# Linear attention and a LoRA mixture-of-experts FFN on one core: stage-1 products split 384 + 280, denominators and spreading on strips of the array, DVE order of a tile rewritten

## The chip, the core and the metric

The kernel runs on one core of a Trainium2 chip. TensorE (PE) multiplies, VectorE (DVE), ScalarE (ACT) and GpSimd (POOL) work beside it, SyncE (SP) issues nearly all DMAs. The metric is the device time of the whole program in microseconds (us); less is better.

## What is computed

`x` is 2 batches of 1024 tokens of 512 numbers, all float32. The reference, cut to what matters:

```python
xn = layernorm(x)
Q, K, V = heads(xn @ wq.T + bq), heads(xn @ wk.T + bk), heads(xn @ wv.T + bv)   # 16 heads of 32
Q, K = elu(Q) + 1.0, elu(K) + 1.0
KV = einsum('bhsd,bhse->bhde', K, V)
QKV = einsum('bhsd,bhde->bhse', Q, KV)
QK_sum = einsum('bhsd,bhd->bhs', Q, K.sum(axis=-2))
attn = (QKV / (QK_sum[..., None] + 1e-8)) @ wo.T + bo

scores = sigmoid(xn @ W_router)                      # 8 experts, two best of scores + bias
w = one_hot(topk_idx) * topk_scores / topk_scores.sum()
gate = xn @ W_gate + shared_lora(xn) + expert_lora(xn, w)
up   = xn @ W_up   + shared_lora(xn) + expert_lora(xn, w)
hidden = silu(gate) * up                             # 1376 wide
out = x + attn + hidden @ W_down + shared_lora(hidden) + expert_lora(hidden, w)
```

## The kernel before, in words

Every float32 operand of a large product is split into a rounded part (`_h`, type fp32r, written by ACT) and a remainder (`_l`, written by DVE as a subtraction). A product is then three matmuls, h times h, h times l, l times h (`product`), 512 columns wide as a rule.

**Stage 1** goes over 16 tiles of 128 tokens. For a tile `t`, PE computes the keys K (12 matmuls of 512 columns), transposes the next tile's normalised tokens (`transpose_tokens(t + 1)`), transposes the LoRA inputs of tile `t - 2` (`lora_transposed`), computes the values V (12 x 512) and the LoRA and router columns A (12 x 152), and multiplies keys by values of tile `t - 1` (`keys_by_values`: 16 small float32 matmuls of 33 columns, written to four strips of 32 partitions in turn). PE starts a tile's K only when DVE has written that tile's `xt_l` (`tokens_lo`, semaphore `xtl_done`).

Each engine has its queue in the order in which the code is written, and an instruction that waits holds all behind it. The parts that matter here:

- DVE in a tile `t`: `compare(t - 1)` (four small operations on the router scores), `select(t - 1)` (waits for POOL's rank), `kb` (keys plus bias, out of PSUM), the statistics of tile `t + 2`, `kf` (waits for ACT's exponential), `tokens_lo(t + 1)`, `lora_weighted(t - 1)` (`zs`, `zf`; waits for POOL's `wtok`), `normalise(t + 2)` (`xn`; waits for POOL's `rstd`), `lora_lo(t - 1)` (`zst`), the copy `zraw` of the A product, and in every second tile the sum `kvacc`.
- POOL in a tile: `rstd` of tile `t + 2`, then `route(t)`: `rden`, the rank (`eq`, `gt`, `rank`), after `select` seven more dependent operations (`ssum` to `wtok`). So `rstd` of tile `t + 2` stands behind the whole of `route(t - 1)`.
- ACT: `krelu`, `kexp`, `xt_h` of the next tile, `zt` (`lora_out`), `vf` (values), `zst` (`lora_hi`), `rexp`.

**Stage 2** goes over 4 groups of 512 tokens. In a group `g`, PE does `queries(g)` (12 matmuls for each of 4 chunks; the first chunk ahead, at the end of group `g - 1`), `attention(g - 1)` in two halves of 24 matmuls, and between the halves `denominators(g)`: four float32 matmuls that accumulate Q times the key sums of 16 heads in 16 partitions of bank 2. DVE then adds the epsilon and takes the reciprocal, ACT rounds it, DVE writes the remainder (`rr`), and PE spreads 16 rows to 4 x 128 (`expand`: one matmul a chunk, chunks 0 and 1, then `queries(g + 1, (0,))`, then chunks 2 and 3, since only two banks are there). DVE multiplies (`scaled`), ACT rounds, POOL takes the remainder (`qn_l`), and attention follows in the next group. In group 0, 20 matmuls that do nothing (`keep_busy`) run while DVE takes the reciprocal. In the last group, DVE also splits the first weights of stage 3 (`split_up(0, 0, 1)`), after `attention(g - 1, (0, 1))` and before the reciprocal.

**Stage 3** is the FFN, 4 groups of 11 chunks: gate and up products, silu, down products. The change leaves it as it is but for its first chunk.

## Time and profile before

| | us |
|---|---|
| median of 3 runs | 721.21 |
| lowest and highest | 720.41 and 721.88 |
| the profiled execution, its own time | 720.7 |
| its span, first to last instruction | 718.9 |

The profile is of one execution. It gives the busy time of each engine, the waits of each engine with what ended them, the chain of work that ended last, and each instruction with its start and duration. Matmuls overlap, so what a matmul costs on PE is read from the chain, where each piece has the time that it adds, and not from its own duration. "issue" is time in which an engine waited for nothing that the profile shows. The granted clock of TensorE is the full one in all 40 slices.

### The profile page before, as it was taken

The numbers are of one execution on the slowest core, as the hardware profiler recorded it, in microseconds if no ns is written. First come the engines' busy times: TensorE is split into PE (matmuls) and PEld (weight loads), VectorE is DVE, ScalarE is ACT, GpSimd is POOL, SyncE is SP. The second block draws the span as 40 slices with busy tenths as digits, with TensorE's granted clock in tenths as the row PEclk, the third lists the DMA queues.
The fourth block names the chain that finished last, engine by engine and source line by source line (L and its number), as shares of the span: only waits on it lengthen the run. The fifth ranks groups of instructions, "written<-read, shape, count | busy, mean of one in ns | idle before, by whom it ended". The sixth has DMA issues, their size and how long they took to land.

```text
span 718.9 us, 10792 instructions
## 1 busy us (share of the span) xinstructions
PE 701.2 (98%) x3690; PEld 563.2 (78%) x3690; DVE 376.2 (52%) x715; ACT 260.7 (36%) x402; POOL 122.3 (17%) x293
## 2 busy tenths in 40 slices
PE   7999999989999999999999999999999999999997
PEld 5788888876776677888888888888888888888886
DVE  5666556677575675444427444336534435544434
ACT  4344334564331432333333333324333224323322
POOL 3554555420642651000000000000000000000000
PEclk9999999999999999999999999999999999999999
DMA  7756656326746635000010500001600001300001
GB/s 241 270 194 195 202 192 210 125 111 251 274 142 236 221 131 217 18 0 0 0 49 37 208 0 0 0 4 54 233 0 0 0 0 58 117 0 0 0 0 60
DMA packets 22755, 72.79 MB, mean 101 GB/s; under 512 B 2688, under 2 KB 2944, under 8 KB 20688
## 3 DMA queue, kind: packets, MB, share of 16 engines
q1 hardware_dynamic: 22560, 72.24, 28.4%
q0 software_dynamic: 176, 0.30, 0.2%
q8 instruction: 11, 0.18, 0.1%
q14 instruction: 8, 0.07, 0.0%
HBM read 51.56 MB, written 20.97 MB: 101 GB/s over the span
## 4 chain that ended last, share of the span: by engine, by line
PE 90%; DVE 4%; issue 2%; POOL 2%; ACT 1%; DMA 1%; SPq 0%; DVEq 0%; POOLq 0%; ACTq 0%
PE bank L1115 19%; PE bank L1116 19%; PE bank L1117 19%; PE bank L1328 17%; PE bank L1303 6%; PE bank L1315 4%; PE bank L1228 2%; DMA w_raw<-in_wkT 1%; PE bank L1180 1%; PE bank L1132 1%; PE bank L1152 1%; PE bank L1144 1%; PE bank L1236 1%; PE bank L1344 0%; PE bank L1346 0%
## 5 line engine op out<-in xcount | busy, mean ns | idle before, releaser
L1115 PE MATMUL bank<-x,up_h 128*128 (+1 forms) x352 | 137.5, 391 | 2.1 <-DVE qf L980 1.2
L1116 PE MATMUL bank<-x,up_h 128*128 (+1 forms) x352 | 137.3, 390 | 0.0
L1117 PE MATMUL bank<-x,up_l 128*128 (+1 forms) x352 | 137.0, 389 | 0.0
L1048 DVE TENSOR_TENSOR hf<-bank,silu 128x512 f32<-128x512 f32 x44 | 30.4, 692 | 162.3 <-issue 142.6
L1115 PEld LDWEIGHTS bank<-x,up_h 128*128 128x128 f32 x352 | 66.1, 188 | 18.8 <-issue 2.1
L597 ACT ACTIVATE hid_h<-hf 128x512 fp32r<-128x512 f32 x44 | 27.8, 632 | 142.9 <-DVE hf L1048 142.9
L1117 PEld LDWEIGHTS bank<-x,up_l 128*128 128x128 f32 x352 | 66.1, 188 | 14.1
L1116 PEld LDWEIGHTS bank<-x,up_h 128*128 128x128 f32 x352 | 66.1, 188 | 13.8
L793 DVE TENSOR_TENSOR up_l<-up_raw,up_h 128x1024 fp32r<-128x1024 f32 x45 | 55.6, 1235 | 31.4 <-ACT up_h L597 31.4
L1328 PE MATMUL bank<-dn_h,hid_h 128*128 128x512 f32 x176 | 69.5, 395 | 0.0
L1328 PE MATMUL bank<-dn_l,hid_h 128*128 128x512 f32 x176 | 69.1, 392 | 0.0
L1328 PE MATMUL bank<-dn_h,hid_l 128*128 128x512 f32 x176 | 68.9, 392 | 0.0
L597 ACT ACTIVATE up_h<-up_raw 128x1536 fp32r (+1 forms) x45 | 66.0, 1474 | 1.5 <-DVE qf L949 1.5
L750 ACT ACTIVATE silu<-bank 128x512 f32<-128x512 f32 x44 | 26.3, 597 | 101.6 <-PE bank L1303 101.5
L1303 PE MATMUL bank<-z,up_h 128*128 128x512 f32 x176 | 54.2, 389 | 0.0
L793 DVE TENSOR_TENSOR hid_l<-hf,hid_h 128x512 fp32r<-128x512 f32 x44 | 30.5, 692 | 33.8 <-ACT hid_h L597 33.8
L597 ACT ACTIVATE dn_h<-dn_raw 128x592 fp32r (+1 forms) x44 | 30.8, 699 | 43.0 <-PE bank L1315 31.4
L793 DVE TENSOR_TENSOR up_h<-up_raw,up_h 64x256 fp32r<-64x256 f32 x90 | 39.5, 439 | 0.6
L793 DVE TENSOR_TENSOR dn_l<-dn_raw,dn_h 128x592 fp32r<-128x592 f32 x44 | 34.1, 775 | 10.4 <-ACT dn_h L597 9.3
L1328 PEld LDWEIGHTS bank<-dn_h,hid_l 128*128 128x128 f32 x176 | 33.0, 188 | 7.6
L1328 PEld LDWEIGHTS bank<-dn_h,hid_h 128*128 128x128 f32 x176 | 33.0, 187 | 7.4
L1328 PEld LDWEIGHTS bank<-dn_l,hid_h 128*128 128x128 f32 x176 | 33.1, 188 | 7.1
(167 smaller groups left out, 1228.3 us busy)
## 6 DMA issues: line engine op xcount, KB each, us to landing
x<-scr_x SPq DMA_DIRECT2D x8, 2048.0 KB, 7.5
up_raw<-in_ffn_up SPq DMA_DIRECT2D x11, 768.0 KB, 5.5
scr_x<-xt SPq DMA_DIRECT2D x16, 512.0 KB, 4.4
xin<-in_x SPq DMA_DIRECT2D x16, 256.0 KB, 5.8
scr_z<-zt SPq DMA_DIRECT2D x16, 256.0 KB, 2.2
x3r<-in_x SPq DMA_DIRECT2D x16, 256.0 KB, 3.5
scr_att<-x3r SPq DMA_DIRECT2D x16, 256.0 KB, 2.1
z<-scr_z SPq DMA_DIRECT2D x4, 1024.0 KB, 5.0
```

What stands on the lines that cost most here:

```text
L597: return nc.scalar.activation(dst, src, ACT.Copy)
L750: nc.scalar.activation(silu[:], ps_g[:], ACT.Silu).then_inc(silu_done, 1)
L793: return nc.vector.tensor_tensor(dst, a, b.bitcast(F32), ALU.subtract)
L1048: nc.vector.tensor_tensor(hf[:], ps_u[:], silu[:], ALU.mult).then_inc(h_done, 1)
L1115: nc.tensor.matmul(dst, lh, rh, start=start, stop=False, **kw)
L1116: nc.tensor.matmul(dst, lh, rl, start=False, stop=False, **kw)
L1117: return nc.tensor.matmul(dst, ll, rh, start=False, stop=stop, **kw)
L1132: last = nc.tensor.transpose(ps_xt[:, k * P:(k + 1) * P], xn[:, k * P:(k + 1) * P], ident[:])
L1228: last = nc.tensor.matmul(ps_den[0:HEADS, :], kcur[:, c, :], qf[:, c, :], start=(c == 0), stop=(c == KD - 1))
L1303: last = nc.tensor.matmul(dst[:], up_h[:, s, col:col + P], z4[:, :, a * 2 + b, :], start=False, stop=(b == 1))
L1315: d = nc.tensor.matmul(ps_zd[0:DNR, :], w[:, s, D:], h[:, s, :], start=(first and i == 0), stop=(last and i == 2), skip_group_check=True)
L1328: d = nc.tensor.matmul(ps_out[j][:], h[:, s, cols], w[:, s, 0:D], start=(first and i == 0), stop=False, skip_group_check=True)
```

## The change

Stage 1: V and A now stand in one set of 664 columns, and are computed as 384 columns (`va`, three quarters of V) and 280 columns (`vz`, the last quarter of V and A) in two banks; `lora_transposed(t - 2)` stands between them, no longer ahead of V. ACT reads the values in two pieces, the second after DVE's `zraw`. `zraw` has two buffers. DVE's order of a tile is another one: `kb` ahead of `compare` and `select`, and `lora_weighted` and `lora_lo` at the end of the tile, behind `normalise` and `zraw`. The split of `wo` is one quarter in each of the last four tiles in place of two in each of the last two. The loop over tile pairs is one turn shorter, with two more tiles written out.

Stage 2: the denominators of chunk `c` go to partitions 32c to 32c + 31 (heads in rows 0 to 15 and again in 16 to 31), with four separate matmuls of 32 columns of weights; the key sums `kcur` are made once a batch on POOL straight from `kvacc`. The reciprocal and the rest work on 128 partitions, the remainder is made with a mask column `lomask` (one more small load), and `expand` takes 32 partitions a chunk as its contraction, into four banks, all four at once. PE's groups 1 and 2 are written out. In the last group the large part of `split_up` stands between the two halves of `attention(g - 1, (0, 1))` on DVE and the small part behind `attention(g - 1, (2, 3))`, with a semaphore `upb_done` of its own.

```diff
-            for dst, name in ((hmask, "headmask"), (hcol, "headcol"), (hrow_raw, "headrow"), (bdn_raw, "b_dn")):
+            for dst, name in ((hmask, "headmask"), (hcol, "headcol"), (hrow_raw, "headrow"), (lomask, "lomask"), (bdn_raw, "b_dn")):
...
+            def key_sums(b):
+
+                pool.wait_ge(kvacc_done, (b + 1) * TB // 2 + 1)
+                tt(kcur[:, b], hcol[:], kvacc[:, b, :, DK:AUG].to_broadcast([P, KD, DK]), ALU.mult).then_inc(kcur_done, 1)
...
 # ACT, stage 1
+                act.wait_ge(va_ready, t + 1)
+                round_to(vf[:, s, 0:KD - 1, :, 0:DK], ps_va.rearrange("p (k h n) -> p k h n", h=HC, n=DK)).then_inc(va_done, 1)
                 if behind(t, 2):
                     lora_out(t - 2)
-
-                act.wait_ge(v_ready, t + 1)
-                round_to(vf[:, s, :, :, 0:DK], ps_v[:].rearrange("p (k h n) -> p k h n", k=KD, h=HC)).then_inc(vf_done, 1)
+                act.wait_ge(zraw_done, t + 1)
+                round_to(vf[:, s, KD - 1, :, 0:DK], ps_vz[:, 0:P].rearrange("p (h n) -> p h n", n=DK)).then_inc(vf_done, 1)
+                nc.scalar.activation(rexp[:], zraw[:, s, NZ - E:], ACT.Exp, scale=-1.0).then_inc(rexp_done, 1)
                 if behind(t, 1):
                     lora_hi(t - 1)
-
-                act.wait_ge(zraw_done, t + 1)
-                nc.scalar.activation(rexp[:], zraw[:, NZ - E:], ACT.Exp, scale=-1.0).then_inc(rexp_done, 1)
...
 # DVE, stage 1
+                dve.wait_ge(k_ready, t + 1)
+                wait(dve, kf_done, t)
+                nc.vector.tensor_tensor(kb[:], ps_k[:], bk_b[:], ALU.add).then_inc(kb_done, 1)
                 if not first:
                     compare(t - 1)
-                    select(t - 1)
-
-                dve.wait_ge(k_ready, t + 1)
-                nc.vector.tensor_tensor(kb[:], ps_k[:], bk_b[:], ALU.add).then_inc(kb_done, 1)
                 if first:
                     tokens_lo(1, 1)
                 if ahead(t, 2):
                     stats_of(t + 2, s, half + 1)
...
+                if not first:
+                    select(t - 1)
 
                 dve.wait_ge(kexp_done, t + 1)
...
-                if not first:
-                    lora_weighted(t - 1)
                 if ahead(t, 2):
                     normalise(t + 2, s)
+                dve.wait_ge(vz_ready, t + 1)
+                nc.vector.tensor_copy(zraw[:, s], ps_z).then_inc(zraw_done, 1)
                 if not first:
+                    lora_weighted(t - 1, 1 - s)
                     lora_lo(t - 1)
-                dve.wait_ge(z_ready, t + 1)
-                nc.vector.tensor_copy(zraw[:], ps_z[:, 0:NZ]).then_inc(zraw_done, 1)
                 if s == 0 and not first:
                     key_values(t - 1, half - 1)
...
 # DVE, stage 2
-                    attention(g - 1, (0, 1))
-                if then is not None:
-                    then()
+                    attention(g - 1, (0,))
+                    if last:
+                        split_up_w(0, 0, 1).then_inc(upl_done, 1)
+                    attention(g - 1, (1,))
...
-                nc.vector.reciprocal(den[0:HEADS, :], den[0:HEADS, :]).then_inc(rden_done, 1)
+                nc.vector.reciprocal(den, den).then_inc(rden_done, 1)
...
-                sub(rr[DK:DK + HEADS, :], den[0:HEADS, :], rr[0:HEADS, :]).then_inc(rr_done, 1)
+                nc.vector.scalar_tensor_tensor(rr[:], rr[:].bitcast(F32), lomask[:], den, ALU.mult, ALU.add
+                                               ).then_inc(rr_done, 1)
...
+                if last:
+                    split_up_b(0, 0).then_inc(upb_done, 1)
...
 # PE, stage 1
+                wait(pe, va_done, t)
+                tile_of(ps_va, s, va_h[:, :, 0:VA], va_l[:, :, 0:VA], split_before=KD if first else None
+                        ).then_inc(va_ready, 1)
                 if behind(t, 2):
                     lora_transposed(t - 2)
-                wait(pe, vf_done, t)
-                tile_of(ps_v[:], s, wv_h, wv_l, split_before=KD if first else None).then_inc(v_ready, 1)
...
-                tile_of(ps_z[:, 0:NZ], s, a_h, a_l).then_inc(z_ready, 1)
+                tile_of(ps_vz, s, va_h[:, :, VA:], va_l[:, :, VA:]).then_inc(vz_ready, 1)
...
 # PE, stage 2
-                    last = nc.tensor.matmul(ps_den[0:HEADS, :], kcur[:, c, :], qf[:, c, :], start=(c == 0), stop=(c == KD - 1))
+                    last = nc.tensor.matmul(ps_den[c * DK:(c + 1) * DK, :], kcur[:, g // GB, c, :], qf[:, c, :], start=True, stop=True)
...
-                for c in cs:
-                    wait(pe, qn_done, g * KD + c - 1)
-                    nc.tensor.matmul(ps_exp[c % 2][:], hrow[:, c, :], rr[:], start=True, stop=True).then_inc(exp_ready, 1)
+                wait(pe, qn_done, g * KD)
+                for c in range(KD):
+                    strip = slice(c * DK, (c + 1) * DK)
+                    nc.tensor.matmul(ps_exp[c][:], hrow[strip, :], rr[strip, :], start=True, stop=True).then_inc(exp_ready, 1)
...
                     gate_or_up(g, n, 0, 1, first=True)
-                    expand(GROUPS - 1, (2, 3))
                     gate_or_up(g, n, 0, 0)
```

Three places of the instruction streams. The first is DVE in a tile of stage 1. In a row stand the line, the operation, what is written and what is read, and what it waits for; `eq` and `gt` are left out, `zf`, `zs` and `zst` are the LoRA inputs. Before:

```order
L829 RECIPROCAL score<-rden_106 128x8 [waits rden1_done]
...
L841 SCALAR_TENSOR_TENSOR sel<-rank,score 128x8 [waits rank_done]
...
L868 TENSOR_TENSOR kb<-bank,bk_b 128x512 [waits k_ready]
...
L880 SCALAR_TENSOR_TENSOR kf<-kb,kexp 128x512 [waits kexp_done]
L793 TENSOR_TENSOR xt<-bank,xt 128x512 [waits xth_done]
L847 TENSOR_SCALAR zs<-zraw 128x16 [waits route_done]
...
L851 TENSOR_TENSOR zf<-zraw,wtok 128x64 x2
L806 TENSOR_SCALAR xn<-xin,mv,rstd 128x512 [waits xt_ready,ln_rstd]
L793 TENSOR_TENSOR zst<-zf,zst 128x2x64 [waits zhi_done,zf_done]
L793 TENSOR_TENSOR zst<-zs,zst 128x2x8
L892 COPY zraw<-bank 128x152 [waits z_ready]
```

The same place on DVE in the changed kernel:

```order
L869 TENSOR_TENSOR kb<-bank,bk_b 128x512 [waits kf_done]
L833 RECIPROCAL score<-rden_103 128x8 [waits rden1_done]
...
L845 SCALAR_TENSOR_TENSOR sel<-rank,score 128x8 [waits rank_done]
L884 SCALAR_TENSOR_TENSOR kf<-kb,kexp 128x512 [waits kexp_done]
L797 TENSOR_TENSOR xt<-bank,xt 128x512 [waits xth_done]
L810 TENSOR_SCALAR xn<-xin,mv,rstd 128x512 [waits xt_ready,ln_rstd]
L892 COPY zraw<-bank 128x152 [waits vz_ready]
L851 TENSOR_SCALAR zs<-zraw 128x16 [waits route_done]
...
L855 TENSOR_TENSOR zf<-zraw,wtok 128x64 x2
L797 TENSOR_TENSOR zst<-zf,zst 128x2x64 [waits zhi_done,zf_done]
L797 TENSOR_TENSOR zst<-zs,zst 128x2x8
```

`kb` has moved ahead of the comparison, `select` stands right before `kf`, and `zs`, `zf` and `zst` have moved behind `xn` and `zraw`.

The second place is PE in group 0 of stage 2, from the denominators (`kcur`) through the filler (`ident_sb`) and the spreading (`hrow`) to the first query products of group 1 (`wq_h`). Before:

```order
L1228 MATMUL bank<-qf,kcur 16x512 x3
...
L1180 MATMUL bank<-ident_sb 128x128 x20
L1236 MATMUL bank<-rr,hrow 128x512 [waits rr_done,hrow_done]
L1236 MATMUL bank<-rr,hrow 128x512
L1115 MATMUL bank<-x_52,wq_h 128x512 [waits qmax_done,x3_in]
...
L1236 MATMUL bank<-rr,hrow 128x512 [waits qn_done,rr_done]
L1236 MATMUL bank<-rr,hrow 128x512 [waits qn_done]
```

PE at the same place in the changed kernel:

```order
L1242 MATMUL bank<-qf,kcur 32x512 x3
...
L1193 MATMUL bank<-ident_sb 128x128 x20
L1251 MATMUL bank<-rr,hrow 128x512 [waits rr_done,hrow_done]
L1251 MATMUL bank<-rr,hrow 128x512 x3
L1127 MATMUL bank<-x_52,wq_h 128x512 [waits qmax_done,x3_in]
```

The spreading is now in one place, ahead of the query products.

The third place is DVE in the last group of stage 2, with the sums of the attention (`x3r`), the split of stage 3's first weights (`up_l`, `up_h`), the reciprocal and the scaling (`qf<-qf,bank`). Before:

```order
L956 TENSOR_TENSOR x3r<-x3r,bank 128x512 [waits xbo_done,att_ready] x2
L793 TENSOR_TENSOR up_l<-up_raw,up_h 128x1024 [waits uph_done]
L793 TENSOR_TENSOR up_h<-up_raw,up_h 64x2x128
L793 TENSOR_TENSOR up_h<-up_raw,up_h 32x2x128
L967 TENSOR_SCALAR qexp<-bank 16x512 [waits den_ready]
L969 RECIPROCAL qexp<-qexp 16x512 [waits dene_done]
L793 TENSOR_TENSOR rr<-qexp,rr 16x512 [waits rrh_done,rden_done]
L956 TENSOR_TENSOR x3r<-x3r,bank 128x512 [waits xbo_done,att_ready] x2
L980 TENSOR_TENSOR qf<-qf,bank 128x512 [waits exp_ready] x4
```

The same place on DVE in the changed kernel:

```order
L959 TENSOR_TENSOR x3r<-x3r,bank 128x512 [waits xbo_done,att_ready]
L797 TENSOR_TENSOR up_l<-up_raw,up_h 128x1024 [waits uph_done]
L959 TENSOR_TENSOR x3r<-x3r,bank 128x512 [waits xbo_done,att_ready]
L991 TENSOR_SCALAR qexp<-bank 128x512 [waits den_ready]
L993 RECIPROCAL qexp<-qexp 128x512 [waits dene_done]
L996 SCALAR_TENSOR_TENSOR rr<-rr,lomask_sb,qexp 128x512 [waits rrh_done,rden_done]
L959 TENSOR_TENSOR x3r<-x3r,bank 128x512 [waits xbo_done,att_ready] x2
L797 TENSOR_TENSOR up_h<-up_raw,up_h 64x2x128
L797 TENSOR_TENSOR up_h<-up_raw,up_h 32x2x128
L1007 TENSOR_TENSOR qf<-qf,bank 128x512 [waits exp_ready] x4
```

The large piece of the split now stands between two attention sums, the two small pieces right before the scaling.

## Rows read from the trace of the kernel before

**Rows 1.** The page, part 1: busy time, share of the span, instructions.

```profile
PE 701.2 (98%) x3690; PEld 563.2 (78%) x3690; DVE 376.2 (52%) x715; ACT 260.7 (36%) x402; POOL 122.3 (17%) x293
```

**Rows 2.** Waits of PE: line, releaser, us in total, times, longest.

```profile
PE bank L1115 <- DVE xt L793: 2.4, 2, 1.5
...
PE bank L1115 <- DVE qf L980: 1.2, 1, 1.2
```

**Rows 3.** Chain that ended last, stage 1: start us, us added, what.

```profile
34.25 0.23 PE bank L1116
...
35.90 0.11 PE bank L1117
36.01 0.39 PE bank L1144 x32
...
44.72 0.24 issue
...
149.21 0.47 PE bank L1115
```

**Rows 4.** Timeline of DVE, tiles 1 to 3: start, us, line, out<-in, [idle <-releaser].

```profile
24.52 0.68 DVE L868 TENSOR_TENSOR kb<-bank,bk_b 128x512 f32<-128x512 f32 x1
...
30.03 0.20 DVE L829 RECIPROCAL score<-rden 128x8 f32<-128x8 f32 x1 [0.56 <-POOL rden L531]
...
32.56 0.17 DVE L841 SCALAR_TENSOR_TENSOR sel<-rank,score 128x8 f32<-128x8 f32 x1 [1.73 <-POOL rank L538]
32.66 0.69 DVE L868 TENSOR_TENSOR kb<-bank,bk_b 128x512 f32<-128x512 f32 x1
...
34.80 0.69 DVE L880 SCALAR_TENSOR_TENSOR kf<-kb,kexp 128x512 f32<-128x512 f32 x1 [0.51 <-ACT kexp L632]
...
36.01 0.17 DVE L847 TENSOR_SCALAR zs<-zraw 128x16 f32<-128x16 f32 x1
...
36.37 0.55 DVE L806 TENSOR_SCALAR xn<-xin,mv,rstd 128x512 f32<-128x512 f32 x1
37.11 0.29 DVE L793 TENSOR_TENSOR zst<-zf,zst 128x128 fp32r<-128x128 f32 x1 [0.20 <-ACT zst L597]
...
37.41 0.31 DVE L892 COPY zraw<-bank 128x152 f32<-128x152 f32 x1
37.63 0.28 DVE L818 TENSOR_TENSOR kvacc<-kvacc,bank 128x132 f32 x1
38.34 0.20 DVE L829 RECIPROCAL score<-rden 128x8 f32<-128x8 f32 x1 [0.43 <-POOL rden L531]
```

**Rows 5.** Timeline of ACT in tile 2.

```profile
36.47 0.42 ACT L597 ACTIVATE zst<-zf 128x256 fp32r<-128x256 f32 x1 [0.24 <-DVE zf L851]
```

**Rows 6.** Timeline of POOL in tile 2.

```profile
30.91 0.32 POOL L534 TENSOR_TENSOR eq<-eq,earlier_sb 128x64 f32<-128x64 f32 x1 [0.91 <-DVE eq L836]
...
32.33 0.20 POOL L538 TENSOR_TENSOR rank<-gt 128x8 f32<-128x8 f32 x1
32.81 0.20 POOL L541 TENSOR_TENSOR ssum<-sel 128x4 f32<-128x4 f32 x1 [0.28 <-DVE sel L841]
...
34.90 0.66 POOL L547 TENSOR_TENSOR wtok<-sel,ssum 128x8 f32 x1 [0.18 <-POOL ssum L546]
```

**Rows 7.** Timeline of PE in tile 1, right behind K.

```profile
21.40 0.60 PE L1132 MATMUL bank<-ident_sb,xn 128*128 128x128 f32 x4
```

**Rows 8.** Chain that ended last, stage 2: start us, us added, what.

```profile
194.53 3.54 PE bank L1228 x8
...
207.22 0.45 PE bank L1236 x2
...
266.50 0.23 PE bank L1115
```

**Rows 9.** Timeline of DVE, stage 2, last group.

```profile
251.56 0.68 DVE L967 TENSOR_SCALAR qexp<-bank 16x512 f32<-16x512 f32 x1 [0.95 <-PE bank L1228]
```

**Rows 10.** Timeline of POOL, stage 2, last group.

```profile
259.78 2.53 POOL L582 TENSOR_TENSOR qn_l<-qf,qn_h 128x512 fp32r<-128x512 f32 x2 [14.26 <-ACT qn_h L597]
```

More of the change, by code:

```diff
@@ L52 @@
 RSCALE = 1.0 / R
-STAGE2_LOADS = 8
-WO_HALF = {TILES - 2: (0, 1), TILES - 1: (2, 3)}
+STAGE2_LOADS = 9
+WO_PART = {TILES - KD + k: k for k in range(KD)}
 ROUTE_STEPS = 10
@@ L343, in tiles @@
             body(1, 0, 1)
[L344 removed]
+            with eng.Fori(0, TILES // 2 - 3) as p:
                 body(2 * p + 2, p + 1, 0)
                 body(2 * p + 3, p + 1, 1)
[L347 removed]
+            for t in range(TILES - 4, TILES):
                 body(t, t // 2, t % 2)
@@ L983, in group @@
                         m_lo(1, (2, 3))
-                    if c == 3 and then is None:
+                    if c == 3 and not last:
                         queries(g + 1, (0,))
@@ L1093, in late_group @@
                 chunk(n + FC - 1, FC - 1, 0, last=True)
-            group(GROUPS - 1, then=lambda: split_up(0, 0, 1))
+            group(GROUPS - 1, last=True)
             split_up(1, 1, 2)
@@ L1276, in group3 @@
                 attention(g - 1, (2, 3))
-                expand(g, (0, 1))
+                expand(g)
                 if more:
                     queries(g + 1, (0,))
-                    expand(g, (2, 3))
-            with pe.Fori(1, GROUPS - 1) as g:
+            for g in range(1, GROUPS - 1):
                 group3(g)
```

143 lines of the change are left out of this document (73 added, 70 removed).

## The prediction

> **What bounds the kernel now.** I read the busy table first, then the waits of PE, then the chain of work that ended last, and last the instructions of single tiles. PE is busy for 701.2 of 718.9 us, 98% [rows 1], so the plain reading is that whatever shortens PE's work shortens the kernel. Its waits are few: the two for `xt` make 2.4 us, the one for the scaled queries (`qf`, line 980) 1.2 [rows 2]. But this says only that the other engines are in time for PE as it is now, not by how much. That must be read from a tile of stage 1. On DVE one tile's first comparison starts at 30.03 and the next one's at 38.34, 8.31 later [rows 4], and on PE the keys by values end at 36.40 and again at 44.72, 8.32 later, with 0.24 of issue at every second tile [rows 3]: 8.44 a tile. In this tile the copy `zraw` starts right behind `zst` and not when its product is there, and `xn` right behind POOL's `rstd`. So a circle through DVE, POOL and ACT turns nearly as slowly as PE: PE is the bound with a tenth or two of a microsecond to spare. Whether the change shortens that circle decides stage 1.
>
> **Stage 1, PE's work.** In the chain a 512-column matmul adds 0.23 us and a 152-column one 0.11 [rows 3], that is 0.45 and 0.74 ns a column: narrow ones pay more. The 12 pairs cost 12 x 0.344 = 4.13 us a tile. 384 + 280 columns are not in the trace. At 0.45 ns a column the pair costs 0.30; at the other end the 280 could cost 0.74 ns a column, 0.21, and the 384 as much as a 512, and nothing would be gained. I take 0.31, nearer to the wide row, since both widths are over half of 512: 0.4 us a tile, 6 us in all, if nothing else binds.
>
> **Stage 1, the circle.** With `kb` at 0, in the changed order:
> - `kb` 0.68, the next starts 0.09 before its end, as `kvacc` does behind `zraw` [rows 4]: 0.60. Comparison to POOL's `eq`: 30.03 to 30.91 = 0.88; `eq` to the end of `rank`: 30.91 to 32.53 = 1.62 [rows 4, 6]; `select` 0.03 later. Sum 3.13.
> - `select` to `xn` is 32.56 to 36.37 = 3.81 [rows 4]. In it POOL does `ssum` to `wtok`, then `rstd` of tile `t + 2`. `wtok` took 0.66 and ended at 35.56, just behind the end of `kf` at 35.49, against 0.20 for other small POOL operations: it was held while `kf` ran [rows 4, 6]. Now `kf` follows `select` at once and holds the first `ssum` instead (+0.40) and frees `wtok` (-0.46). I keep 3.75.
> - `xn` to `zraw` 0.46 (0.55 less 0.09), `zraw` to `zs` 0.22, `zs` to ACT's `zst` 0.46 (36.01 to 36.47), ACT's to DVE's `zst` 0.64, and 0.30 to the next instruction [rows 4, 5]. Sum 2.08.
> Together 8.96 us; in every second tile `kvacc` and the wait for its end add 0.31. Mean 9.12 a tile against 8.4.
>
> What makes it longer is the order. Before, `kb`, the statistics and `kf` ran in the shade of POOL's routing, and the LoRA steps ahead of `xn` in the same shade. Now `kb` stands ahead of the comparison (+0.60), and `zs` to `zst` stand behind `xn`, which itself waits for POOL to finish the whole route. The second `zraw` buffer takes `rexp` and `rden` out of the circle (0.93 from `zraw` to the next comparison, 37.41 to 38.34), but that is less. PE waits for `xt` once a tile, some 1.2 us: the shortened products and the later LoRA transposes win nothing, and the wait is the price of the order. ACT's second half of `vf` comes 0.35 behind `zraw` and doesn't bind.
>
> Sum: tile 1's `kb` stood at 24.52 behind `select`, though K had ended at 21.40 [rows 4, 7]. It moves to about 21.3, since the first tile's products are a little shorter. Then 7 x 8.96 + 6 x 9.27 = 118.3 to `kb` of tile 14; 0.3 each for the quarters of `wo_l` in tiles 12 and 13, which hold POOL's rank; 0.2 at each of 5 loop ends, as on PE (0.24 of "issue") [rows 3]. That is 141.2. Tile 14 has no `xn`, but `zs` waits for `wtok`: 3.44 to `select`, 2.94 to `wtok`, 0.6 more since `kvm` runs beside POOL, 1.4 to the end of `zst`, 0.3 for `kvacc`: 8.7. In tile 15 `wtok` ends at 6.4, ACT's `zst` starts at 6.9, behind it ACT rounds the transposed heads (to 7.9), DVE takes the remainder (to 8.65), PE starts: 8.9. So the first product of stage 2 starts at 158.8 in place of 149.21 [rows 3]: **+9.6 us**. An error of 0.15 in the circle is 2 us here.
>
> **Stage 2, denominators.** 4 matmuls, 8 pieces, add 3.54 us [rows 8], 0.885 each, on the path in each of 4 groups. On four strips they can run side by side. Bounds: 0.885 (all at once) and 3.54 (in turn). The nearest row are the keys by values, 32 pieces of 33 columns to four strips in 0.39 [rows 3]. At the denominators' 0.86 ns a column they would take 0.91 in turn, so strips do overlap, 2.3 times, and by that the denominators would be 1.5. But those pieces are so short (12 ns each) that issue may set them. I take 1.05, near the lower bound: -2.5 us a group. DVE works on 128 partitions in place of 16, which costs nothing by the rows (0.68 for 16 x 512, 0.69 for 128 x 512 [rows 4, 9]). Its chain from the denominators to `rr` is as long as before and lies beside the same work, attention's second half or the filler, so all of the gain reaches the end: **-10.0**. The Trainium skill (TensorE: Matmul & The Clock Gate, "Part 3: Packing small matmuls") gives three column strips of N = 512 a measured 2.38 times and four row strips 3.07 times; by the latter, an estimate, the denominators would be 1.15 and the sum 0.4 us worse.
>
> **Stage 2, spreading.** Two matmuls add 0.45 in the stream [rows 8], so four 0.90. In strips, with 32 partitions each, between 0.23 and 0.90, and no row shows strips of the contraction. I take 0.35: -0.55 in groups 0 to 2, **-1.65**. `key_sums` on POOL is free: between two routes for batch 0, and behind the last route for batch 1, whose user is group 2. The added small load goes to SP long before its use.
>
> **Last group.** From DVE's first step on the denominators at 251.56 to the first attention product behind the gate at 266.50 are 14.94 us [rows 8, 9], the 1.2 of wait in it. Afterwards, counted from that step: the scaling, which stood at about 6.75, starts 0.85 later, behind the two small splits of 256 columns (some 0.42 each, estimated from 0.68 for 512), at 7.6. POOL's first `qn_l` starts 1.48 behind it (scaling and rounding), at 9.1, and the four take 1.27 each (2.53 for two [rows 10]), to 14.2: attention starts at 14.3, **-0.6**. The wait for the queries goes, and POOL's is late next. The split's large piece would have delayed the reciprocal, now that the denominators are short, by up to 1.1; its move avoids that.
>
> **Sum.** +9.6 - 10.0 - 1.65 - 0.6 = -2.65. The profiled execution's own time is 720.7, so 718.05; the median of the runs is 0.5 above it, so **718.6** as a median.
>
> **Rivals.**
> - *Stage 1 is held by PE after all* (my circle is too long, say because POOL isn't held by `kf`, or `xn` waits less). At the old 8.4 a tile stage 1 costs nothing and the time is 709; with the full 0.4 a tile and K of tile 2 starting 2 us earlier it is 701. For it: 98% busy. Against it: `xn` right behind `rstd` in rows of before. 14%.
> - *The circle is still longer.* The Trainium skill (SBUF — State Buffer, "SBUF: two separate sides") says that DVE and GpSimd share a port pair that the first comer locks for its whole instruction; the trace agrees for `wtok` behind `kf` [rows 4, 6]. If more of POOL's operations are held than I count (the rank by the statistics, the last ones by `xt_l`), 0.3 a tile adds 4: 722.5, on the other side. It decides from 0.2 a tile. 13%.
> - *Strips don't overlap*: the four denominators keep 3.54 and the spreading 0.9. Then stage 2 gains 0.6 only and stage 1's loss stands: 730. Against it the keys by values. Half an overlap: 723. 9%.
> The forecast's own case has 64%, 714.5 to 722.
>
> **How the numbers follow.** A run of this kernel can tell 0.2%, 1.4 us, from no change. Faster (below 719.8): 0.52 of the 0.64 and all of the first rival, 0.66. Same: 0.10 and a part of the others, 0.16. Slower: 0.18. The range leaves out the lower half of the first rival and the upper half of the third: 709 to 724.
>
> **What would show it.** Right: PE in stage 1 waits for `xt` once a tile, together 12 to 18 us; comparison to comparison on DVE about 9.1; the product after the last tile at 159; `kcur` pieces about 1.05 a group in the chain, and a group of stage 2 some 3 us shorter. Wrong: tiles of 8.0 to 8.4 without waits (first rival), or `kcur` pieces over 2 us (third).

## Result: 0.45% slower, and the profile after

The changed kernel takes **725.84 us** as a median of 7 runs (724.54 to 726.18); the kernel before takes 721.92 in 7 runs beside them (720.41 to 723.62). The ratio, of the two means, is 1.0045, with a 95% interval of 1.0029 to 1.0061. Forecast were 718.6, 0.4% faster than the median of 721.21 that was known then, and it became 0.45% slower. The profiled execution spans 723.8 us, before 718.9; this difference, 4.9, is larger than that of the medians, 3.9. One reason is under "The clock" below: the profiled execution of before is one of its quick ones.

Waits of PE in the changed kernel (engine, line waited for: us in total, times, longest); before, `xt` made 2.4 us in two waits [rows 2]; "..." stands for lines left out, here and in all that follows:

```profile
PE bank L1127 <- DVE xt L797: 18.6, 15, 1.8
...
PE bank L1164 <- DVE zst L797: 2.5, 1, 2.5
PE bank L1127 <- POOL qn_l L591: 1.5, 1, 1.5
...
PE bank L1127 <- DMA x<-scr_x: 0.7, 1, 0.7
PE bank L1127 <- DVE qf L1007: 0.4, 1, 0.4
```

So PE waits for `xt` in 15 of the 16 tiles, as forecast. What PE does in between is shorter, also as forecast. Timeline of PE in tile 2: the second and the eleventh product of 384 columns, and the same of 280:

```profile
30.93 0.34 PE L1128 MATMUL bank<-va_l,xt 128*128 128x384 f32 x1
...
32.51 0.34 PE L1128 MATMUL bank<-va_l,xt 128*128 128x384 f32 x1
...
33.43 0.29 PE L1128 MATMUL bank<-va_l,xt 128*128 128x280 f32 x1
...
34.59 0.29 PE L1128 MATMUL bank<-va_l,xt 128*128 128x280 f32 x1
```

Nine steps take 1.58 and 1.16 us: 0.176 and 0.129 a product, a pair 0.304 (estimate 0.31, before 0.344 [rows 3]).

The circle of the same tile. First DVE, then POOL (start, duration; in brackets the idle time ahead and what ended it); compare [rows 4 to 6]:

```profile
31.79 0.69 DVE L869 TENSOR_TENSOR kb<-bank,bk_b 128x512 f32<-128x512 f32 x1
...
34.93 0.17 DVE L845 SCALAR_TENSOR_TENSOR sel<-rank,score 128x8 f32<-128x8 f32 x1 [0.80 <-POOL rank L546]
35.02 0.68 DVE L884 SCALAR_TENSOR_TENSOR kf<-kb,kexp 128x512 f32<-128x512 f32 x1
...
38.84 0.55 DVE L810 TENSOR_SCALAR xn<-xin,mv,rstd 128x512 f32<-128x512 f32 x1 [2.54 <-POOL rstd L520]
...
39.53 0.16 DVE L851 TENSOR_SCALAR zs<-zraw 128x16 f32<-128x16 f32 x1
...
40.63 0.29 DVE L797 TENSOR_TENSOR zst<-zf,zst 128x128 fp32r<-128x128 f32 x1 [0.67 <-ACT zst L603]
...
41.24 0.69 DVE L869 TENSOR_TENSOR kb<-bank,bk_b 128x512 f32<-128x512 f32 x1
```

```profile
35.18 0.58 POOL L549 TENSOR_TENSOR ssum<-sel 128x4 f32<-128x4 f32 x1 [0.28 <-DVE sel L845]
...
37.66 0.21 POOL L555 TENSOR_TENSOR wtok<-sel,ssum 128x8 f32 x1 [0.18 <-POOL ssum L554]
37.99 0.19 POOL L518 TENSOR_TENSOR vare<-mv,epsln 128x1 f32<-128x1 f32 x1
38.26 0.55 POOL L520 TENSOR_TENSOR rstd<-vare,mhalf 128x1 f32<-128x1 f32 x1
```

`kb` to `kb` is 9.45 us in this even tile, 9.22 in tile 1 (22.57 to 31.79); the mean of tiles 1 to 13 is 9.46, and the kernel before needed 8.32 there. DVE stands idle 2.54 us ahead of `xn`, because POOL computes `rstd` only behind the route, and the LoRA steps (`zs` to `zst`, with 0.67 of idle for ACT) stand behind that wait.

Stage 2. PE's four denominators, DVE's reader of them, and the spreading, in group 2; compare [rows 8, 9]:

```profile
231.23 1.07 PE L1242 MATMUL bank<-qf,kcur 128*32 128x512 f32 x8
232.23 0.50 PE L1127 MATMUL bank<-m_h,qn_h 128*128 128x512 f32 x1
```

```profile
232.37 0.69 DVE L991 TENSOR_SCALAR qexp<-bank 128x512 f32<-128x512 f32 x1 [0.34 <-PE bank L1242]
```

```profile
238.01 0.51 PE L1251 MATMUL bank<-rr,hrow 32*128 32x512 f32 x4
238.45 0.50 PE L1127 MATMUL bank<-x,wq_h 128*128 128x512 f32 x1
```

The denominators take 1.00 of PE's stream (3.54 before), the spreading 0.44 (0.90). A group takes 23.80 us from spreading to spreading (214.21 to 238.01), before 26.74.

Where the 4.9 us come from, by marks in the two profiled executions:

| stretch | before | after | difference | forecast |
|---|---|---|---|---|
| start to `kb` of tile 1 | 24.52 | 22.57 | -1.95 | -3.2 |
| to the first product of stage 2 | 124.69 | 140.18 | +15.49 | +12.8 |
| to the first denominators | 18.41 | 19.59 | +1.18 | 0 |
| to the first spreading | 9.41 | 7.28 | -2.13 | -2.5 |
| to the second denominators | 17.43 | 17.81 | +0.38 | -0.55 |
| to the fourth denominators | 53.46 | 47.63 | -5.83 | -6.1 |
| to DVE's last addition to `x3r` | 29.50 | 27.57 | -1.93 | -3.1 |
| to the end | 441.48 | 441.17 | -0.31 | 0 |
| sum | 718.9 | 723.8 | +4.9 | -2.65 |

Two groups of errors are to be explained: stage 1 (the first two stretches) is 3.9 us worse than forecast, stage 2 is 3.6 worse.

### The profile page after: what moved, and what is told of

It is laid out like the page before. It is cut to its first block, busy times and chain, and to the rows that moved or that the text cites. A ratio compares the mean times of both kernels' runs of the same rounds, so it can differ in the third digit from the quotient of the medians.

```text
span 723.8 us, 10757 instructions
## 1 busy us (share of the span) xinstructions
PE 688.7 (95%) x3690; PEld 559.9 (77%) x3690; DVE 375.7 (52%) x712; ACT 260.9 (36%) x418; POOL 121.3 (17%) x291
## 4 chain that ended last, share of the span: by engine, by line
PE 63%; issue 15%; POOL 14%; DVE 3%; DMA 2%; ACT 2%; POOLq 1%; SPq 0%; DVEq 0%; ACTq 0%
PE bank L1342 17%; PE bank L1127 12%; PE bank L1128 12%; PE bank L1129 12%; PE bank L1317 5%; PE bank L1329 4%; POOL x3r L585 2%; POOL qn_l L591 2%; POOL ssum L554 1%; POOL gt L545 1%; POOL ssum L549 1%; DMA x<-scr_x 1%; POOL rstd L520 1%; DMA w_raw<-in_wkT 1%; POOL eq L542 1%
## 5 line engine op out<-in xcount | busy, mean ns | idle before, releaser
L1127 PE MATMUL bank<-wk_h,xt 128*128 128x512 f32 x64 | 27.4, 428 | 18.6 <-DVE xt L797 18.6
L1127 PE MATMUL bank<-va_h,xt 128*128 128x384 f32 (+1 forms) x128 | 43.0, 336 | 0.0
L1129 PE MATMUL bank<-va_h,xt 128*128 128x384 f32 (+1 forms) x128 | 40.3, 315 | 0.0
L1128 PE MATMUL bank<-va_l,xt 128*128 128x384 f32 (+1 forms) x128 | 40.3, 315 | 0.0
```

The costliest lines, as they stand in the source:

```text
L1127: nc.tensor.matmul(dst, lh, rh, start=start, stop=False, **kw)
L1128: nc.tensor.matmul(dst, lh, rl, start=False, stop=False, **kw)
L1129: return nc.tensor.matmul(dst, ll, rh, start=False, stop=stop, **kw)
```

## Experiments

Each ratio is against the kernel before on the same chip, with its 95% interval. Differences to the changed kernel are of medians that were partly taken on other chips; where the ratios say something else, the text gives it. The expectations name other runs by number: the first is stage 2 alone, the fourth `rstd` taken out of the way, the eighth the LoRA steps one tile later, the ninth the same with SP in step.

**Stage 2 alone, and stage 1 alone.** The first kernel is the one before with all edits of stage 2 (`kcur` and `rr` on strips, `key_sums`, the split of the last group). The second is the changed kernel with stage 2 as before.

> Stage 2 of the changed kernel (denominators, spreading and the scaled reciprocals on strips, key sums once a batch, last group's split moved) behind stage 1 of the kernel before. Theory A (the loss of the change lies in stage 1, and stage 2 gains what was forecast, 10.0 + 1.65 us): first stage-2 product at 149 as before, a group of stage 2 at 23.8 instead of 26.8, and a time of 710 to 711.5 us. Rival B (the strips lose something that the two traces hide, at the step into stage 2 or in the last group, so that part of the loss is theirs): 713 to 718.

> Stage 1 of the changed kernel in front of stage 2 of the kernel before: the complement of the run beside it. Theory A: the first stage-2 product comes at 163 instead of 149.2 and the time is 721.9 + 13.5 to 15 = 735.5 to 737 us. Rival B: less than 732, since part of the loss stays with the strips. If the two halves don't interact, the two differences to the kernel before add up to that of the whole change (+3.9).

Measured: 714.78 us, ratio 0.988 (0.9855 to 0.9905), and 733.78 us, ratio 1.0153 (1.013 to 1.0176). So the whole loss is stage 1's, about 11 us, and stage 2 gains 8 to 9, not the 12.25 forecast. The two differences add up to +2.4, against +3.9 of medians or +3.2 by the ratio for the whole change; with intervals of some 2 us on each this shows no interaction, and would not show one of a microsecond. Theory A holds for the sign; for the size of stage 2's gain rival B was right. The second kernel, with its first product of stage 2 at 161.89, lies between its two branches (735.5 to 737, and below 732). The trace of the first kernel shows two places. PE, behind the first spreading, waits for a load, and SP issued that load only behind its last store of `z`:

```profile
178.76 0.51 PE L1247 MATMUL bank<-rr,hrow 32*128 32x512 f32 x4 [0.16 <-DVE rr L993]
180.58 0.50 PE L1124 MATMUL bank<-x,wq_h 128*128 128x512 f32 x1 [1.31 <-DMA x<-scr_x]
```

```profile
147.25 24.34 SPq L385 DMA_DIRECT2D scr_z<-zt  x3
171.64 0.43 SPq L379 DMA_DIRECT2D x<-scr_x  x1
```

The second place is the clock at the step into stage 2, below.

**DVE's order put back.**

```
 if not first:
     compare(t - 1)
+    select(t - 1)
 kb[:] = ps_k + bk_b                 # and no select behind the statistics
 ...
+lora_weighted(t - 1, 1 - s)
 normalise(t + 2, s)
+lora_lo(t - 1)
 zraw[:, s] = ps_z
-lora_weighted(t - 1, 1 - s)
-lora_lo(t - 1)
```

> The changed kernel with DVE's order in stage 1 as before (comparison and selection ahead of kb; the LoRA weighting ahead of xn, its remainder ahead of zraw; ACT's rounding of zst ahead of its second part of vf). The widths 384 + 280, both zraw buffers, the later LoRA transposes and the strips stay. Theory A (the order of DVE and POOL sets the tile): 8.3 to 8.4 us a tile as before, since DVE's circle then was 8.31; first stage-2 product at 149 to 150.5, time 709.5 to 712. Rival C (the 384 + 280 split itself, with vf and v in two parts, or the late LoRA transposes lengthen the tile): tiles of 8.8 to 9.3 and 717 to 725. Rival D (PE was the bound and the narrower pair helps once the order is right): 8.0 a tile and 705.

Measured: 713.96 us, ratio 0.9874 (0.985 to 0.9898), 11.9 below the changed kernel. A tile takes 8.42 us, the first product of stage 2 comes at 151.11. The edit moves ACT's `lora_hi` back too, ahead of its second part of `vf`. The order costs the 1 us a tile; widths, the two-part `v` and the late transposes don't (rival C falls). They aren't free in this order, though: the first seven tiles of the kernel before, where `kb` waits for nothing but the selection, take 8.21 in the mean, so the circle is 0.2 longer here. Most of it lies between `zraw` and the next comparison, 1.03 and 1.10 in place of 0.87 and 0.93, since ACT now rounds the last quarter of the values ahead of `rexp`. Rival D falls too: with this order the circle takes 8.4 itself and PE still waits 10.3 us in all for `xt`.

**Half of the order put back:** `kb` stays ahead of the comparison, only the LoRA steps return ahead of `xn` and `zraw` (the second half of the diff above), and ACT's `lora_hi` with them.

> The changed kernel with half of DVE's order as before: kb stays ahead of the comparison and the selection behind the statistics, but the LoRA weighting stands ahead of xn and its remainder ahead of zraw again (and ACT's rounding of zst ahead of its second part of vf). It tells which half of the new order costs. Theory A1 (the LoRA steps in a row behind xn, which itself waits for POOL's whole route, are the cost): 3.1 to the selection, 3.9 to xn, 0.5, and 0.3 + 0.25 + 0.15 behind it = 8.2 to 8.3 a tile, 1.1 to 1.2 less than the changed kernel: 708.5 to 711. Rival A2 (kb ahead of the comparison is the cost, 0.6, and the other half is small): 8.8 to 9.0 a tile, 717 to 720.

Measured: 712.31 us, ratio 0.9855 (0.9827 to 0.9884). Tiles of the loop alternate between 8.02 and 8.53 us, 8.28 in the mean: theory A1. DVE in its tile 2:

```profile
33.27 0.17 DVE L845 SCALAR_TENSOR_TENSOR sel<-rank,score 128x8 f32<-128x8 f32 x1 [0.80 <-POOL rank L546]
...
36.23 0.17 DVE L851 TENSOR_SCALAR zs<-zraw 128x16 f32<-128x16 f32 x1 [1.58 <-POOL wtok L555]
...
37.18 0.55 DVE L810 TENSOR_SCALAR xn<-xin,mv,rstd 128x512 f32<-128x512 f32 x1 [0.45 <-POOL rstd L520]
37.64 0.29 DVE L797 TENSOR_TENSOR zst<-zf,zst 128x128 fp32r<-128x128 f32 x1
...
38.47 0.69 DVE L869 TENSOR_TENSOR kb<-bank,bk_b 128x512 f32<-128x512 f32 x1
```

Selection to `xn` is 3.91 here as in the changed kernel, but `zs` and `zf` now fit between `wtok` and `rstd`, and ACT's `zst` beside `xn`. All of the loss is this one pair of edits with the move of `lora_hi` that goes with it; no run has one of the three alone. `kb` ahead of the comparison, with the selection behind the statistics, is even 0.14 a tile better in the loop than the old place (8.28 against 8.42); the times' intervals overlap.

**`rstd` taken out of the way.** On POOL, in the changed kernel:

```
 tt(rank[:], ...).then_inc(rank_done, 1)
+rstd_of(t + 3)                      # was behind the whole route
 pool.wait_ge(sel_done, t + 1)
```

> The changed kernel with one move: POOL computes rstd of the tile two ahead between the rank and the sums of the route, not behind the whole route, so that xn no longer waits for it. Theory A (circle): xn starts right behind the low part of the tokens, selection to xn falls from 3.9 to some 2.0 us, and the circle is then closed by wtok (0.5 later than now): 3.1 to the selection, 3.4 to wtok, 1.4 to the end of zst, 0.15 for kvacc = 8.1 to 8.2 a tile, PE at 8.0 to 8.1 close behind; stage 1 loses 1.1 us a tile against the changed kernel, 15 us: 709 to 713. If POOL's steps ahead of wtok cost more than they take out of the way: 8.6 a tile, 715 to 718. Rival C (widths, two-part vf, late transposes set the tile): 724 to 726, no change.

Measured: 714.38 us, ratio 0.9888 (0.9864 to 0.9912); 8.66 a tile. DVE in tile 6:

```profile
68.51 0.68 DVE L800 TENSOR_TENSOR xt<-bank,xt 128x512 fp32r<-128x512 f32 x1
69.11 0.54 DVE L813 TENSOR_SCALAR xn<-xin,mv,rstd 128x512 f32<-128x512 f32 x1
...
71.55 0.17 DVE L854 TENSOR_SCALAR zs<-zraw 128x16 f32<-128x16 f32 x1 [1.68 <-POOL wtok L557]
...
72.73 0.29 DVE L800 TENSOR_TENSOR zst<-zf,zst 128x128 fp32r<-128x128 f32 x1 [0.67 <-ACT zst L606]
```

`xn` waits for nothing now, and `wtok` takes its place, as the second branch of the expectation had it (8.6 a tile; the time is 0.6 below its 715 to 718). From the selection to the end of `wtok` are 3.68 us in place of the changed kernel's 2.94: `rstd`'s steps stand ahead of the sums, and their `pow` takes 0.98 instead of 0.55 while DVE runs `kf`.

**The LoRA steps one tile later.** On DVE (ACT's and PE's LoRA steps move along, and POOL has `rstd` as in the run above):

```
 stats_of(t + 2, s, half + 1)
+lora_weighted(t - 2, s)
 select(t - 1)
 ...
 normalise(t + 2, s)
+lora_lo(t - 2)
 zraw[:, s] = ps_z
-lora_weighted(t - 1, 1 - s)
-lora_lo(t - 1)
```

> The changed kernel with the LoRA weighting and its roundings one tile later (that of tile t - 2 in tile t, which the second zraw buffer allows: the weighting on DVE between the statistics and the selection, its remainder behind xn), PE's LoRA transposes behind those of the tokens, and rstd between the rank and the sums, as in the fourth run. In the fourth run DVE still waited in every tile 1.68 us for wtok, 0.67 for ACT's zst and 0.8 to 0.9 for the rank: 8.66 a tile. Theory A (a circle through DVE, POOL and ACT sets the tile, and the 384 + 280 pair is worth what was estimated): without wtok in the circle DVE's own chain is 3.2 to the selection and 3.1 behind it, 6.3 to 6.6, so that PE binds: 8.47 less 0.45 = 8.0 to 8.1 a tile, no wait for xt; first stage-2 product at 144 to 146 (in the last tile the weighting of tile 14 remains), time 706 to 709. Rival C (the two-part v or the new pieces hold the tile): 8.4 or more a tile, 712 or more.

> The eighth kernel (LoRA weighting one tile later) with SP's queue in step: the store of z of tile t - 3 in tile t, not of t - 2. In the eighth run the first tiles took 7.67 to 7.96 us and then 8.2, and 11.5 in tile 12 to 13, where the store of z, which waits for ACT's zt a tile later now, held the token store and the next load behind it on SP's queue (statistics waited 0.9 to 1.5 for xin, ACT 1.4 to 3.4 for the token store). Theory Q (that queue is the whole of it, and then PE binds): 7.9 to 8.0 a tile from 4 to 13, no wait of ACT for the token store, kb of tile 15 at 134 to 136 in place of 139.5, time 710 to 712. Rival (something else holds the tile at 8.2): 714 to 715.

Measured: 715.1 us, ratio 0.9893 (0.9861 to 0.9925), and with SP's stores of `z` in step 708.03, ratio 0.9799 (0.9773 to 0.9826). The first of the two was a miss by 6 us: the mechanism worked in tiles 1 to 3 (7.67, 7.78, 7.96) and then SP's queue held the loads. Waits of ACT and DVE from 20 to 130 us, in the first:

```profile
ACT xt L608 <- DMA scr_x<-xt: 13.4, 7, 3.4
DVE stats L809 <- DMA xin<-in_x: 7.8, 7, 1.5
```

and in the second, all waits of this kind:

```profile
ACT xt L612 <- DMA scr_x<-xt: 1.2, 1, 1.2
DVE stats L813 <- DMA xin<-in_x: 0.3, 1, 0.3
```

Tiles take 7.98 us in the mean, 8.05 in pairs of the loop, and `kb` of tile 15 comes at 134.13: theory Q, with a time 2 below its 710 to 712. DVE now waits for PE's K. That is PE's own time with 384 + 280 columns: 0.42 less than its 8.47 in the later tiles of the kernel before, against 0.4 estimated. (From tile 1 to tile 8 `kb` advances by 8.21 a tile only: it starts 3.1 us behind the end of K in tile 1, at 24.52 against 21.40 [rows 4, 7], and this distance is used up there.) The wait came from a step that was moved a tile later, with a queue that issued in the order of before: a store waiting for it held two transfers behind it.

**The clock.** The changed kernel with 6 more small products of the identity in front of its first product, and 3 and 5 at the two waits ahead of stage 2:

```
-keep_busy(ps_t, 4)
+keep_busy(ps_t, 10)
 ...
+keep_busy(bank[4], 3)
 lora_transposed(TILES - 2)
+keep_busy(bank[4], 5)
```

> The changed kernel with more filler products of the identity where PE waits: 10 instead of 4 ahead of the first product of the kernel, and 3 and 5 at the two waits in front of stage 2. In the changed kernel 8 products of the first tile and 6 to 8 behind the last tile ran at half their speed (granted clock at its half level there), behind waits of 1.8 and of 2.5 and 0.3 us; the kernel before waited 0.9 at the start and showed no such products. Theory K (the waits let the clock fall, and that is part of the loss): no product at half speed, granted clock 1.0 in 9 to 18 and 160 to 170, and 1.5 to 3.5 us shorter: 722.5 to 724.5. Rival (the clock there falls for other reasons, or the gain is lost in waits behind): 725.8.

Measured: 723.29 us, ratio 1.0011 (0.9998 to 1.0025), 2.5 below the changed kernel and inside theory K's range. Stretches (length; busy time of PE, PEld, DVE, ACT, POOL; granted clock; DMA share; GB/s), first of the changed kernel, then of this one:

```profile
9.00:18.00 9.00, 7.42 (x29) 5.93 (x30) 8.05 (x16) 4.99 (x10) 0.75 (x2) 0.81 0.67 166
160.00:170.00 10.00, 8.17 (x33) 6.59 (x33) 7.65 (x20) 6.52 (x14) 0.36 (x2) 0.83 0.16 59
```

```profile
9.00:18.00 9.00, 7.83 (x44) 6.27 (x43) 7.93 (x16) 4.97 (x10) 0.75 (x2) 1.00 0.76 215
160.00:170.00 10.00, 8.93 (x48) 7.61 (x49) 8.42 (x19) 7.82 (x16) 0.00 (x0) 1.00 0.11 42
```

In the changed kernel PE had waited 1.82 us ahead of its first product (0.93 in the profiled execution of before), and 2.49 ahead of the LoRA transposes of tile 14. Behind each, products took 0.43 from start to start where they take 0.23:

```profile
161.83 1.07 PE L1164 MATMUL bank<-ident_sb,zst 128*128 128x128 f32 x4 [2.49 <-DVE zst L797]
...
163.32 0.63 PE L1128 MATMUL bank<-wo_l,kvt_h 128*128 128x512 f32 x1
163.74 0.63 PE L1129 MATMUL bank<-wo_h,kvt_l 128*128 128x512 f32 x1
```

That is the lower of the clock's two levels, 1.2 in place of 2.4 GHz. The kernel before has it too in some executions: the stage-2-only kernel, whose code up to there is that of before, lost 1.5 us between its first product of stage 2 and its first denominators (19.87 against 18.41), with waits of 0.8 and 1.22 where the one of before shows 0.59 and 1.22 and no fall. So part of that is chance, from run to run. The stage-1-only kernel waited 1.80 us ahead of its first product and 2.48 us at the later place, as the changed one did, and shows no product at the lower level at all. And of 19 executions of the kernel before that ran beside these experiments on one chip, five took 720.3 to 721.4 with a mean granted clock of 0.999 or 1.0, as the profiled one did (720.7, 1.0); the other 14 took 722.2 to 724.8, 13 of them at 0.994 to 0.997. The changed kernel's seven were at 0.992 to 0.998. So the kernel before pays for the clock in most executions too, and only a part of this term can be put down to the change.

Where the gain comes from is told by the marks of the table above; the two traces differ by 1.8. From the first product of stage 2 to the first denominators are 18.44 us in place of 19.59: 1.15, the clock. To the second denominators from the first spreading are 17.14 in place of 17.81: there PE doesn't wait for its load in this execution, 0.7. `kb` of tile 1 comes 0.53 earlier, but not by the fillers. The weights landed 0.5 earlier in this execution, and from ACT's first rounding of the values' weights to `kb` of tile 1 are 9.4 us in both kernels, since PE at its full rate then waits 1.2 us for DVE's remainder of those weights (`va_l`). So the lower clock in the first tile cost nothing, and the fillers there won nothing. At the step `kb` of tile 15 to the first product takes 9.43 in place of 8.84, the price of the fillers.

**Load and fillers in the stage-2-only kernel.** On SP `x3_load(1)` moves ahead of `store_z(TILES - 1)`, and the fillers 3 and 5 are added.

> The kernel of the first run (stage 2 with strips, stage 1 as before) with two edits at the step into stage 2: SP loads the tokens of group 1 ahead of the last store of z, not behind it; and PE fills its two waits there with small products of the identity (3 and 5). In the first run PE waited 1.3 us for the load of group 1, and 14 products behind the step took twice their time, at the granted clock's half level, 1.4 to 1.5 us. Theory L (the gain of the first group's denominators was given back to that load, queued behind a store that waits for POOL's, ACT's and PE's last LoRA steps): the wait goes, first denominators' end to second denominators is 17.4 less 0.5 = 17 us instead of 18.4. Theory K (waits at the step let the clock fall): no half-level products behind the step. Both: 714.8 less 1.3 to 2.8 = 712 to 713.5. If neither, 714.8; fillers that come too late for their waits add up to 0.5.

Measured: 711.64 us, ratio 0.9855 (0.9818 to 0.9893), 3.1 below the stage-2-only kernel, or 1.8 by the ratios, whose intervals overlap. The traces tell more. The load is issued at 165.14 in place of 171.64 and the wait is gone: from the first spreading to the second denominators 17.05 us, before the edit 18.39; no product at the step runs at the lower level, where 8 did before the edit (the expectation's 14 was a wrong count; its 1.5 us stands). The two stretches are 1.3 and 1.5 us shorter, so both theories hold in the traces.

**The last group.** In the changed kernel POOL's four `qn_l` end last; the experiment puts the four on DVE, behind the scaling:

> The changed kernel with the last group's four qn_l subtractions on DVE, behind the scaling, in place of POOL. In the changed kernel they take 6.00 us on POOL, 265.36 to 271.36, and PE waits 1.5 for them. Theory H (POOL is what is late in the last group: its four at 1.27 each, and the first held 0.9 by DVE's scaling): DVE does the four in about 2.5 us, PE's gate product (end 269.9) binds instead, and the last group is shorter by the whole 1.5. Rival (the copies and the second up split behind them on DVE become late): gain under 0.5, with a new wait of PE for up_l or x3r.

The first and the last of POOL's four in the changed kernel, and DVE's scaling and its next split beside them:

```profile
265.36 1.28 POOL L591 TENSOR_TENSOR qn_l<-qf,qn_h 128x512 fp32r<-128x512 f32 x1 [12.91 <-ACT qn_h L603]
...
269.10 2.26 POOL L591 TENSOR_TENSOR qn_l<-qf,qn_h 128x512 fp32r<-128x512 f32 x1
```

```profile
263.87 2.48 DVE L1007 TENSOR_TENSOR qf<-qf,bank 128x512 f32<-128x512 f32 x4
268.43 1.81 DVE L797 TENSOR_TENSOR up_l<-up_raw,up_h 128x1024 fp32r<-128x1024 f32 x1 [2.08 <-ACT up_h L603]
```

The four in the experiment:

```profile
266.40 2.49 DVE L798 TENSOR_TENSOR qn_l<-qf,qn_h 128x512 fp32r<-128x512 f32 x4
```

Measured: 723.98 us, ratio 1.0015 (0.9999 to 1.0032), 1.9 below the changed kernel; in the traces 1.76 from the fourth denominators to the last addition, and PE's attention follows the gate without a wait. Theory H, by the traces; the intervals of the two ratios touch. But the reason in the expectation for the 6.00 on POOL in place of 4 x 1.27 = 5.1 [rows 10] is wrong. The first piece ran beside DVE's scaling and took 1.28; the second and third took 1.31 and 1.3. The fourth alone is long, 2.26: it started at 269.10, when DVE's split of the next weights (`up_l`, from 268.43) was running. In the kernel before, the fourth `qn_l` started 0.7 ahead of that split and took 1.30, and the split took 1.70 where it takes 1.2 by itself.

A further kernel puts the up split back in one piece ahead of the reciprocal.

> The changed kernel with the up split of the last group put back: in one piece, weights and small parts, ahead of the last group's reciprocal. Theory A (the move is worth something, as forecast: up to 1.1 us of delay of the reciprocal avoided): attention of the last group starts 0.5 to 1.1 later, counted from the last denominators. Rival G (the move wins nothing, since the small pieces hold the scaling afterwards by as much): within 0.2 of the changed kernel's 16.35 us from the last denominators (255.06) to the attention behind the gate (271.41).

Measured: 725.94 us, ratio 1.0047 (1.0027 to 1.0066). The reciprocal starts 1.5 later behind the denominators, PE waits 1.6 for `rr` (and 8 products behind this wait run at the clock's lower level), attention starts 0.76 later and the last group is 0.62 longer in the trace (28.19 against 27.57); the times can't tell that apart. Theory A, in one trace: the move saves a good half of the 1.1 that the forecast gave as its upper bound.

**All together:** the LoRA steps a tile later with SP in step, those of tile 14 behind the first products of stage 2, the load, DVE's `qn_l` and fillers (10 at the start, 5 ahead of stage 2); tiles 2 and 3 are written out.

> All that the runs pointed to, in one kernel: the ninth kernel, the last tile's LoRA steps of tile 14 behind the first products of stage 2, the load of group 1 ahead of the last store of z, the last group's qn_l on DVE, and fillers at the start and ahead of stage 2. Sum, from the changed kernel's 725.8: stage 1 at 7.95 instead of 9.45 a tile over 13 tiles, -19; the step into stage 2 (kb of tile 15 to the first product 8.8, before 6.9) at 6.5, -2.3; load -0.8; last group -1.8; clock -1.5 to -3. Together 698 to 702. If PE's new waits at the step eat the gain: 703 to 706.

Measured: **702.51 us** (701.78 to 703.7), ratio 0.9722 (0.9699 to 0.9744): 2.8% faster than the kernel before, and between the two ranges of the expectation. Busy time of PE, and its longest waits:

```profile
PE 685.1 (98%) x3712; PEld 560.8 (80%) x3712; DVE 378.0 (54%) x716; ACT 260.3 (37%) x418; POOL 120.3 (17%) x287
```

```profile
PE bank L1215 <- DMA ident_sb<-in_ident: 3.7, 1, 3.7
PE bank L1184 <- DVE zst L810: 1.5, 2, 0.8
PE bank L1264 <- DVE qf L966: 1.4, 1, 1.4
```

## Why the prediction was wrong

**Right, with its mechanism.** PE stopped being the bound of stage 1 and waited for `xt` in 15 of 16 tiles, 18.6 us (12 to 18 forecast; 1.8 of it is the start). The order was the reason: `zs` to `zst` behind an `xn` that waits for POOL's route. The pair of 384 + 280 columns (0.304 for 0.31), the denominators (1.00 for 1.05), the spreading (0.44 for 0.35), a group of stage 2 (-2.94 for -3.05) and the up split's move (0.6, up to 1.1 forecast) came as said. The room that it gave the circle was a little too small: "a tenth or two" a tile, where the kernel before has PE at 8.47 and the circle at 8.21.

**Step 1 that failed: the size of the circle.** Forecast 8.96 and 9.27, measured 9.22 and 9.45 in tiles 1 and 2; in the loop, where the forecast adds 0.2 at each end of a turn, 9.46 to 9.54 for 9.16 and 9.46 for 9.27. In tile 2 `kb` to selection is 3.14 (3.13 forecast), `xn` to the next `kb` 2.40 (2.39); nearly the whole error is in "I keep 3.75" for selection to `xn`, which took 3.91. Behind the held `ssum`, `wtok` ends 2.94 behind the selection, as in the kernel before (3.00); but `vare` then starts 0.12 behind `wtok`'s end, which it did not while `wtok` was held, and `xn` comes 0.97 behind `wtok`'s end in place of 0.81. Thirteen tiles make 2 us of that. The start gave 1.3 more: `kb` of tile 1 at 22.57 and not 21.3, since ACT could start on the values' weights at 13.17 only, 1.24 later than in the trace of before. That is the luck of the loads: other runs with this start have `kb` of tile 1 between 21.18 and 22.65. The 8 products of the first tile at the lower clock have no part in it ("The clock" above). The rest, 0.6, is spread over the loop's turns and the tiles with `wo_l` (0.9), less 0.3 in tiles 14 and 15. This was the second rival, "the circle is still longer", with 0.23 a tile in all (3.0 us from `kb` of tile 1 to `kb` of tile 14); it had 13%, though the text itself said that 0.15 is 2 us. Its mechanism was only half right: POOL's rank and its last sums were not held longer; what was missing is the 0.16 between `wtok` and `xn`.

**Step 2 that failed: "so all of the gain reaches the end".** Of the 12.25 in stage 2, 8.6 arrived. Four pieces make up the 3.6; the 0.3 lost in groups 1 and 2 and the 0.3 won behind the last addition cancel:
- In group 0 the denominators gained 2.1 and not 2.5. There PE waits on DVE's chain to the spreading, and DVE, which had found the denominators unfinished before (its step began 3.63 behind their start), now still computes `m_l` when they are done: its step begins 1.55 behind their start, in group 2 1.14.
- Queries of group 1 came earlier, and their load did not: it stood behind a store on SP. The stretch is 0.9 worse than forecast, 0.7 of it this wait (1.3 in the stage-2-only kernel). The forecast looked at PE, DVE and POOL there, and not at SP's queue.
- The clock at the step: 1.2 between these two executions. In most others the kernel before pays it too, so this piece is in part luck of the execution that the forecast started from.
- The last group gained 1.9 and not 3.1. POOL was rightly named as late next, but with 1.27 for each of its four `qn_l`; the fourth took 2.26, beside DVE's split of the next weights, which now started ahead of it. With it attention starts 15.11 behind DVE's first step in place of 14.3; 0.1 more is missing at that step (1.24 behind the denominators' start, 1.14 in group 2), and 0.3 lies behind attention's first product. The same rows [rows 4, 6] that showed `wtok` held behind `kf` should have been applied to that split. The Trainium skill (SBUF — State Buffer, "SBUF: two separate sides") says that DVE and GpSimd share a port pair, and that a DVE instruction with two inputs in SBUF locks it against GpSimd's reads for its whole length if it starts first. Here the trace agrees: beside the split, which reads two tiles of SBUF, `qn_l` took 2.26, and beside the scaling, which reads one of its two inputs from a PSUM bank, 1.28.

The sign turned on sums of terms of 10 us each way, with 2.65 left between them; errors of 0.2 us a tile and 0.9 a group were enough. The range ended at 724, below the 725.84 that came, and had no place for the clock and the load. The load follows from PE arriving early at a place where it now waits. For the clock the runs don't show how much of it the new waits bring, and how much is there in most executions of either kernel.

## What to carry to other kernels

An engine at 98% may have a circle of other engines turning close behind it (0.26 us a tile here). Before moving steps there, write down the circle with each idle time and its releaser; put a step whose input arrives early into the idle time of another, and never behind a wait that is later than its own. Here one pair of edits in DVE's order cost 13 us, and the same buffer that the change had added allowed the steps a tile later, with `rstd` moved up, for 18 less.

When a step moves to a later tile, move with it whatever waits for it on a queue (SP's store here: 7 us by the medians, 6 in the traces); and when an early stage gets shorter, look for the next group's load and ask behind what it is issued.
